# Last shared tile at the batch's end, maxima split and selection moved; router's weights written ahead of q's parts and operands

## What is computed

```python
xn = _layernorm(x)
x = x + attn(xn) + ffn(xn)
# attn: 16 heads of 8, causal softmax, output projection, then
out = jnp.where(jnp.isnan(out), 0, out)
# ffn: 8 experts of width 176, the best 2 of a softmax of logits,
combine = topk_w / (topk_w.sum(-1) + 1e-20) * 2.5
y = sum_e combine[e] * ((silu(x @ wg[e]) * (x @ wu[e])) @ wd[e])
# and a shared one of width 352, not weighted
return y + (silu(x @ swg) * (x @ swu)) @ swd
```

## Time and profile before

| | |
|---|---|
| median of 3 runs | 626.02 us (625.43 to 626.56) |
| profiled execution | 626.13 us, of which the trace's span is 624.4 us |
| PE busy | 538.2 us (86%) |
| DVE busy | 479.1 us (77%) |
| ACT busy | 349.7 us (56%) |
| POOL busy | 342.8 us (55%) |
| chain that ended last | PE 53%, DVE 17%, issue 12%, ACT 10%, POOL 4%, DMA 2% |
| TensorE's granted clock | 0.973 of full, mean |

### The profile page before, as it was taken

How to read it: one execution, slowest core, us unless ns; L and a number is a source line. 1 busy time by engine, 2 the same in 40 slices (tenths; PEclk the granted TensorE clock), 3 DMA queues, 4 the chain that set the end, 5 groups by cost and what they waited for, 6 DMA issues and landing times.

```text
span 624.4 us, 13266 instructions
## 1 busy us (share of the span) xinstructions
PE 538.2 (86%) x4568; PEld 299.7 (48%) x4568; DVE 479.1 (77%) x784; ACT 349.7 (56%) x478; POOL 342.8 (55%) x358
## 2 busy tenths in 40 slices
PE   2627989988899979998899979999899988999794
PEld 1315742655336642565436653466426653466322
DVE  5947988897968977798868978789767979589412
ACT  5412398353983459533883359633793359633591
POOL 5155734484346845387345944477354864378342
PEclk9968999998999999999999999999999999999896
DMA  8645023700345004710246004610138003530000
GB/s 272 177 154 132 2 72 120 202 3 0 123 125 163 2 21 140 196 51 0 82 135 190 0 6 136 199 66 0 62 124 214 7 3 121 169 118 3 20 1 17
DMA packets 43197, 56.65 MB, mean 91 GB/s; under 512 B 4544, under 2 KB 28576, under 8 KB 43168
## 3 DMA queue, kind: packets, MB, share of 16 engines
q1 hardware_dynamic: 40800, 53.56, 28.8%
q10 hardware_dynamic: 2368, 2.70, 1.3%
HBM read 41.05 MB, written 14.81 MB: 89 GB/s over the span
## 4 chain that ended last, share of the span: by engine, by line
PE 53%; DVE 17%; issue 12%; ACT 10%; POOL 4%; DMA 2%; SPq 0%; DVEq 0%; POOLq 0%; ACTq 0%
PE banks L608 10%; PE banks L505 7%; ACT probs L805 7%; PE banks L470 6%; PE banks L486 5%; PE banks L581 5%; DVE neg_max L1140 5%; PE banks L472 5%; PE banks L471 5%; PE banks L488 3%; PE banks L487 3%; DVE probs L1122 2%; DVE not_nan L1197 2%; POOL probs L885 2%; POOL hid_lo L891 1%
## 5 line engine op out<-in xcount | busy, mean ns | idle before, releaser
L1140 DVE TENSOR_REDUCE neg_max<-banks 128x2 f32<-128x1024 f32 (+3 forms) x224 | 195.0, 916 | 28.1 <-PE banks L496 26.4
L805 ACT ACTIVATE probs<-banks 128x1024 f32<-128x1024 f32 x160 | 155.4, 1030 | 8.1 <-PE banks L581 5.8
L891 POOL TENSOR_TENSOR hid_lo<-probs,hid_hi 128x512 fp32r<-128x512 f32 (+1 forms) x88 | 113.6, 1291 | 75.1 <-ACT hid_hi L760 75.1
L885 POOL TENSOR_TENSOR probs<-probs,cb 128x512 f32<-128x512 f32 x88 | 113.0, 1284 | 73.8 <-ACT probs L753 66.7
L919 POOL TENSOR_SCALAR_AFFINE_SELECT probs<-probs 128x512 f32<-128x512 f32 x128 | 88.8, 717 | 112.3 <-ACT probs L805 112.3
L753 ACT ACTIVATE probs<-banks 128x512 f32<-128x512 f32 (+1 forms) x112 | 66.8, 597 | 134.2 <-PE banks L472 134.2
L760 ACT ACTIVATE hid_hi<-probs 128x512 fp32r<-128x512 f32 (+1 forms) x112 | 70.4, 628 | 80.2 <-DVE probs L1122 79.9
L470 PE MATMUL banks<-x_hi,w_hi 128*128 128x512 f32 (+1 forms) x224 | 95.0, 424 | 11.7 <-DVE probs L1122 10.8
L1122 DVE TENSOR_TENSOR probs<-probs,banks 128x512 f32<-128x512 f32 (+1 forms) x112 | 75.4, 680 | 33.6 <-POOL probs L885 29.2
L608 PE MATMUL banks<-probs,v_op 128*32 128x512 f32 (+3 forms) x1024 | 95.2, 444 | 0.4
L471 PE MATMUL banks<-x_lo,w_hi 128*128 128x512 f32 (+1 forms) x224 | 88.6, 396 | 0.0
(11 more groups left out here) (120 smaller groups left out, 590.3 us busy)
## 6 DMA issues: line engine op xcount, KB each, us to landing
cb<-c_dram SPq DMA_DIRECT2D x32, 256.0 KB, 4.2
q_op<-q_dram SPq DMA_DIRECT2D x32, 192.0 KB
k_op<-k_dram SPq DMA_DIRECT2D x32, 192.0 KB
cb<-c_dram SPq DMA_DIRECT2D x16, 224.0 KB, 4.6
q_dram<-q_parts SPq DMA_DIRECT2D x8, 384.0 KB, 2.5
k_dram<-k_parts SPq DMA_DIRECT2D x8, 384.0 KB, 2.6
cb<-c_dram SPq DMA_DIRECT2D x16, 192.0 KB, 4.1
cb<-c_dram SPq DMA_DIRECT2D x16, 160.0 KB, 4.3
```

Source lines behind the costliest of these rows:

```text
L805: nc.scalar.activation(probs[:, g % 2, 2 * u:2 * u + 2, :], ring[:, at:at + 2, :], ACT.Exp).then_inc(exp_done, 1)
L885: nc.gpsimd.tensor_tensor(sg[k % 3][:, :], sg[k % 3][:, :], cb[:, TILE_ORDER[k], :], ALU.mult).then_inc(weighted, 1)
L891: nc.gpsimd.tensor_tensor(hid_lo[0:n, k % 3, :], hid[k % 3][0:n, :], hid_hi[0:n, k % 3, :].bitcast(F32), ALU.subtract).then_inc(hid_lo_don ...
L1140: return nc.vector.tensor_reduce(out, in_, AX.X, ALU.max, negate=True)
```

## The change

The NaN selection no longer touches `base` and `both`. DVE adds the experts' result into x's own place (`x_sb`). `att` is a buffer of its own, POOL sets `clean` to zero, DVE copies `att` into it where it is a number, and POOL adds `clean` to `x_sb` at the start of the next experts stage; the store of batch i - 1 stands in SP's list of batch i, ahead of the maxima. Find and copy stand on DVE at the end of attention, behind `normalise_o`, no longer ahead of the last `hidden`. Exp 0 of attention waits for that `hidden` no more.

From batch 1 on, the order of tiles is 11, 12, the eleven routed ones, 13, so the last tile is shared. On DVE the maxima are split one `hidden` later. DVE also makes the high part of the last two tiles. ACT copies k behind the first exp instead of ahead of it; PE forms the transposed scores 0 ahead of the projections of v and the logits.

DVE's and SP's orders in attention change as the rows below show. In the prologue the low parts of the routed gate and up weights are both made by DVE, v's bias has a semaphore of its own, the router's weights go out on ACT's queue, and three pairs of maxima stand ahead of `hidden` 3.

Of the diff, in the order SP, PE, ACT, POOL, DVE in experts, DVE in attention:

```diff
+TILES_FIRST = list(range(ROUTED, NT)) + list(range(ROUTED))
+TILES_LATER = list(range(ROUTED, NT - 1)) + list(range(ROUTED)) + [NT - 1]
...
             def weights_out(j):
...
                 sp.wait_ge(comb_written, 16 * j + 16)
+                apart(sp, sp_passed)
...
             def batch(i):
                 k_parts_out(i + 1)
                 q_parts_out(i + 1)
+                weights_out(i + 1)
                 operands_in(i + 1, i, 0)
-                weights_out(i + 1)
                 for m in range(len(CB_GROUPS)):
                     weights_around(m)
                 operands_in(i + 1, i, 1)
+                if not (isinstance(i, int) and i == 0):
+                    store(i - 1)
                 maxima_in(i + 1)
-                store(i)
-                sp.wait_ge(stored, 16 * i + 16)
...
...
                         if front:
                             project_k(b + 1)
+                        scores_t(b, 0, 0)
+                        if front:
                             project_v_and_logits(b + 1, vl)
-                        scores_t(b, 0, 0)
...
-                            if (g, u) == (2, 3):
+                            if (g, u) == (1, 3):
                                 transpose_comb(i + 1)
...
                     if k == NT - 2:
+                        high_hidden(b, k - 1)
                         if front:
                             take_xT(b + 1)
...
-                    if k >= 1:
+                    if 1 <= k < NT - LATE_HIGH:
                         high_hidden(b, k - 1)
+                    if i is None and k == 3:
+                        weights_out()
...
-                        if n == 0:
-                            act.wait_ge(hid_done, NT * i + NT)
...
                             if (g, u) == (0, 0):
+                                take_k(i + 1)
                                 exp_router(i + 1)
...
+                if i is not None:
+                    if not (isinstance(i, int) and i == 0):
+                        add_clean(i - 1)
+                    clear(i)
...
                 for k in range(NT + 1):
-                    if k == 4 and i is not None:
-                        add_attention(i)
-                    if k == NT and i is not None:
-                        find_numbers(i)
-                        finish_output(i)
-                    if k >= 1:
+                    if k >= 1 and not (k == 4 and i is None):
                         hidden(b, k - 1)
+                    if k >= 1 and n == NAT_ALL and pairs_at[k - 1]:
+                        split_maxima(b)
...
+                        if k == 3 and m == 1 and i is not None:
+                            add_attention(i)
                         pair(b, i, n)
                         n += 1
-                    if n == NAT_ALL and pairs_at[k]:
-                        split_maxima(b)
+                    if k == 4 and i is None:
+                        hidden(b, 3)
                     if k >= NT - LATE + 2:
+                        if k - 2 >= NT - LATE_HIGH:
+                            high_hidden(b, k - 2)
                         low_hidden(b, k - 2)
+                high_hidden(b, NT - 1)
+                low_hidden(b, NT - 1)
                 if front:
                     router_logits(b + 1, vl)
-                low_hidden(b, NT - 1)
...
                     take_v(i + 1, vl)
                     split_k(i + 1)
+                    router_weights(i + 1)
                     split_q(i + 1)
+                    take_combT(i + 1)
                 add_tokens(i)
                 if front:
-                    router_weights(i + 1)
-                    take_combT(i + 1)
                     split_x(i + 1, xnT[:, :])
...
                 normalise_o(i, 0)
                 if second:
                     statistics(3)
+                else:
+                    find_numbers(i - 1)
+                    finish_output(i - 1)
```

More of the change, by code:

```diff
@@ L77, in rows_of, with tiles_of, routed_through @@
     return LAST if tile == NT - 1 else P
+def tiles_of(b):
+    return TILES_FIRST if isinstance(b, int) and b == 0 else TILES_LATER
+def routed_through(b, k):
+    return sum(t < ROUTED for t in tiles_of(b)[:k + 1])
 def expert_segments():
@@ L445, in gate_up @@
             def gate_up(b, k):
-                tile = TILE_ORDER[k]
+                tile = tiles_of(b)[k]
                 n = rows_of(tile)
@@ L895, in experts, with clear, add_clean @@
             def experts(b, i):
-                for k in range(NT - ROUTED - 1):
-                    low_hidden(b, k)
-                if i is None:
-                    low_down()
-                place_v(b, i)
-                for k in range(NT - ROUTED, NT):
-                    if k == NT - ROUTED + 2 and i is not None:
-                        sum_all(i)
-                    for m, tiles in enumerate(CB_GROUPS):
-                        if TILE_ORDER[k] == tiles[0]:
+                tiles = tiles_of(b)
+                if i is not None:
+                    if not (isinstance(i, int) and i == 0):
+                        add_clean(i - 1)
+                    clear(i)
+                for k in range(NT):
+                    for m, group in enumerate(CB_GROUPS):
+                        if tiles[k] == group[0]:
                             pool.wait_ge(cb_loaded[m], 16 * len(SEGMENTS[m]) * (b + 1))
-                    weigh_hidden(b, k)
-                    if k - 1 < NT - LATE:
+                    if tiles[k] < ROUTED:
+                        weigh_hidden(b, k)
+                    if 1 <= k <= NT - LATE:
                         low_hidden(b, k - 1)
-            def sum_all(i):
-                pool.wait_ge(tail_step, 3 * i + 1)
-                nc.gpsimd.tensor_tensor(both[:, :, :], att[:, :, :], base[:, :, :], ALU.add).then_inc(summed, 1)
+                    if k == 2:
+                        if i is None:
+                            low_down()
+                        place_v(b, i)
+            def clear(i):
+                before(pool, summed, i)
+                apart(pool, pool_passed)
+                nc.gpsimd.memset(clean[:, :, :], 0.0).then_inc(cleared, 1)
+            def add_clean(i):
+                own = x_sb[:, bass.ds(i * QT, QT), :]
+                pool.wait_ge(tail_step, 3 * i + 3)
+                nc.gpsimd.tensor_tensor(own, own, clean[:, :, :], ALU.add).then_inc(summed, 1)
             def mask(view):
@@ L960, in _ @@
             attend(NB - 1)
-            sum_all(NB - 1)
+            add_clean(NB - 2)
+            clear(NB - 1)
         @block.vector
@@ L1032, in split_qk @@
             def split_qk(j, n, taken, parts, step, written):
-                whole, rest = qk_f[:, n, :], qk_rest[:, n, :]
+                whole, rest = qk_f[:, n, :], qk_rest[:, :]
                 dve.wait_ge(taken, j + 1)
@@ L1203, in finish_output, with add_last @@
                 apart(dve, dve_passed)
-                dve.wait_ge(summed, i + 1)
+                dve.wait_ge(cleared, i + 1)
                 apart(dve, dve_passed)
                 apart(dve, dve_passed)
-                nc.vector.copy_predicated(base[:, :, :], not_nan[:, :, :], both[:, :, :]).then_inc(tail_step, 1)
+                nc.vector.copy_predicated(clean[:, :, :], not_nan[:, :, :], att[:, :, :]).then_inc(tail_step, 1)
+            def add_last():
+                own = x_sb[:, (NB - 1) * QT:NB * QT, :]
+                dve.wait_ge(tail_step, 3 * NB)
+                dve.wait_ge(summed, NB - 1)
+                nc.vector.tensor_tensor(own, own, clean[:, :, :], ALU.add).then_inc(summed, 1)
             def pair(b, i, n):
```

91 lines of the change are left out of this document (45 added, 46 removed).

## The result

The changed kernel takes 650.6 us (648.0 to 654.1), the kernel before 625.7 on the same chip: 1.040 times as long, 95% interval 1.035 to 1.045. I had forecast 635.8 us and a range of 615 to 646. The direction was right; the size was 24.9 us instead of 9.8, and outside the range.

What follows compares the result with a forecast made beforehand. ACT paces attention, PE then PE with DVE pace experts, which end in a chain. On the 624.4 us span, - 15.1 - 2.8 - 0.2 - 5.7 + 23.1 + 10.5 = +9.8 gave 634.2, so 635.8 us measured; range 615 to 646.

Steps and rivals of the forecast that it cites:

- The mechanism of the loss: Attention: the router's instructions ahead of q's parts and the weights' write ahead of the operands make PE's first pair wait.
- the stall: PE idle ahead of its first pair, waiting for the operands: 3.3 us in each of seven batches, 23.1 us more.
- from the operands' first issue until they can be used: 8.84 us: Attention, ahead of PE's first pair: operands usable 8.84 us after first issue, as in the prologue; at most 8.81 in the loop.
- the stretch up to exp 3 of the first batch: Prologue and batch 0: 5.7 us gained in the prologue, 1.1 lost with PE's new order; 4.6 less.
- all that follows the pairs: Everything from PE's first pairs on, end of experts' gains against clock loss included: 8.7 us less.
- The prologue: Before the loop: earlier weights' write, `cb` and maxima gain 5.7 us, with bounds of 3 and 7.
- The lower bound of 3 us: Prologue: gain only 3 us if the write waits for the operands' traffic and `cb` comes at 41.7 or later.
- The clock: Behind PE's stall the granted clock falls to 0.50, costing 1.5 us in each of seven batches, 10.5 us.
- Rival 1: Behind the stall ahead of PE's first pair, the clock holds: 625.3 us, range 620 to 628; chance 16%.
- The end of experts: From the split of the maxima to exp 3: exps start earlier, 2.2 us less six times; 15.1 less together.
- `add_attention`: Moved into an idle gap of DVE in experts' PE-paced part: 0.4 us less in 7 batches, 2.8.
- Rival 2: Attention's operands come in time for PE's first pair; find and copy cost 1.4 us seven times: 612 us; chance 14%.

Runs made afterwards that it cites:

- experiment 1: Changed kernel with the attention stage back in the old order on DVE, SP and PE: 614.4 us, 0.981 of the kernel before.
- experiment 2: Changed kernel with SP's order alone undone, operands ahead of the weights' write: 639.9 us, 1.025 of the kernel before.
- experiment 4: Changed kernel with DVE's order and PE's transposition in attention undone, SP's order kept: 656.4 us, 1.047 of the kernel before.
- Experiment 3: Changed kernel with SP holding the `cb` reads until the first operands have landed: 643.6 us, 1.029 of the kernel before.
- experiment 9: Kernel before with one edit, the split of the maxima behind the last-but-one `hidden`: 614.4 us, 0.982 of the kernel before.
- experiment 10: Kernel before with the attention part of the change alone, on DVE, SP and PE: 669.7 us, 1.071 of the kernel before.
- experiment 8: From experiment 1, prologue's weights' write back on SP's queue, constants and `hidden` 3 at their old place: 613.0 us, 0.978 of the kernel before.
- experiment 11: Changed kernel with 14 unused matmuls on PE ahead of the wait for the operands: 640.1 us, 1.022 of the kernel before.
- experiment 6: From experiment 1, the split of the maxima again ahead of the last-but-one `hidden`: 628.1 us, 1.004 of the kernel before.
- experiment 7: From experiment 1, a routed tile last in every batch, as in the kernel before: 612.8 us, 0.978 of the kernel before.
- experiment 5: From experiment 1, find and copy moved from the end of attention into the first part of experts: 615.8 us, 0.982 of the kernel before.
- experiment 12: From experiment 1, the normalising of the tokens moved behind the sixth pair's place: 624.3 us, 0.997 of the kernel before.

## Why the prediction was right in direction and wrong in size

**The mechanism of the loss was right.** The stall ahead of PE's first pair stands where it was put, with a DMA as releaser. q's parts were to come 7.9 us behind exp 3 (8.16 in the batch shown, 7.4 in the mean), the operands 4.3 later (4.3). Experiments 1, 2 and 4 show both orders as its cause.

**The term that was mis-sized is the stall: 3.3 us forecast, 4.4 measured**, seven times (23.1 against 30.7 us from exp 3 to the pair). The step that failed is "from the operands' first issue until they can be used: 8.84 us". It is 10.3 in the mean of the seven batches, while q's parts come 0.5 us sooner than forecast. I took the 8.84 from rows 8 and 6, where nothing or only a small write follows the operands. In the changed order the write is ahead, so nothing holds the `cb` reads back any more, and they enter the DMA engines 3.1 us behind the operands' first issue. Experiment 3 puts them back behind and gets 8.8 us instead of 10.3. The forecast counted every instruction that was moved, but not what the moved wait had been keeping away: the write's wait on SP was the fence between operands and `cb`.

This is half of the error. On the span 9.8 us more were forecast and 24.6 measured: the seven stalls are 7.6 us of the difference, the stretch up to exp 3 of the first batch 3.5 (4.6 less forecast, 1.1 less measured), all that follows the pairs the rest (8.7 less forecast, 5.0 less measured), and this last is mainly the clock.

**The prologue: 5.7 us forecast, nothing measured.** SP's queue, ACT's queue, PE and POOL there, which answer to rows 8:

```profile
31.07 1.19 ACTq L776 DMA_DIRECT2D c_dram<-combT  x1
...
35.62 2.22 SPq L361 DMA_DIRECT2D cb<-c_dram  x5
...
37.92 0.64 PE L515 MATMUL banks<-k_op,q_op 48*64 48x384 bf16 x8 [1.15 <-DVE neg_max L1167]
42.21 1.26 POOL L903 TENSOR_TENSOR probs<-probs,cb 128x512 f32<-128x512 f32 x1 [7.66 <-DMA cb<-c_dram]
```

The write left at 31.07, as forecast, but took 4.56 us beside the operands' reads, not 2.75, and from the `cb` issue to the first product it was 6.6 us, not 5.0: POOL starts at 42.21, 0.8 us sooner than before, not at 39.3. In the ten traces with this order it starts at 42.2 to 44.4, in the kernel before and experiments 9 and 10 at 43.0 to 43.6, so not even the 0.8 us is a gain. The lower bound of 3 us, for a `cb` later than 41.7, named the case but not the price. PE's third pair did move, from 46.27 to 37.92; with POOL's first product where it was, that was worth nothing in experiment 8 (third pair at its old place behind `hidden` 3, POOL at 42.34).

The Trainium skill, page "DMA: Bandwidth & Descriptors", section "Queues, rings and completion order", gives the rule that engines take turns between queues. The measured write shows how little that is worth here. With nothing beside it the write takes 2.6 us (252.67 to 255.24), behind the reads on the same queue 4.9 to 6.3 in the kernel before, and beside them on the other queue 4.6 to 6.7 in the ten traces; in eight of these SP issues the `cb` reads, which wait for the write, within 0.1 us of the first pair, which waits for the operands. So the write landed about when the reads did, although it had a queue of its own. Why, no run shows.

**The clock: 10.5 us forecast.** The mechanism is shown by the granted clock of 0.50 to 0.74 behind the seven first pairs, and by experiment 11, where filling the wait gave back 10.5 us in all. The term was too small: 1.5 us per batch forecast, 2.2 by the batches of experiment 11 and 2.1 by experiment 10. In seven batches that is some 5 us, about what is missing behind the pairs. Rival 1, that the clock holds, is out for this kernel, where it fell seven times of seven.

**The end of experts: right in size, wrong in its causes.** 2.2 us per batch forecast, 2.05 to 2.2 in the trace. Experiments 6 and 9 show that the order of split and `hidden` is nearly all of it. The last shared tile brings nothing (experiment 7). That exp 0 no longer waits for find and copy shows at exp 0 (306.55 in experiment 6, 11.95 us behind the maxima, against 13.07), but k's copy behind it and, with find and copy in attention, the wait at the third pair take it back. In the changed kernel that loss is hidden by the stall, as forecast. `add_attention`, 2.8 us forecast, cannot be seen apart: all after the pairs is 5.0 us less, where the forecast (without the prologue and the first batch) had 8.7 less. The batch ahead of the loop has a share in that: from its first pair to the next exp 3 it takes 59.4 us, 1.1 more than before (58.3), where the loop's batches take 0.5 less (53.1 against 53.6). Its split takes 4.2 us instead of 2.4, and exp 1 starts 3.8 us behind exp 0 instead of 1.5. The long split is not the reason: experiment 1 has it as well (4.2 us), and there exp 1 starts 2.2 us behind exp 0 and the stretch takes 56.2 us. What this trace has of its own is the granted clock between the two exps, 0.58 from 163 to 167 us against 1.00 in experiment 1. Why it fell there is open.

**Rival 2** (operands in time: 612 us) is in effect experiment 1, at 614.4. Its price for find and copy, 1.4 us per batch, is more than its own numbers give (1.77 and 0.7 less 1.3 make 1.2). Measured are a wait of 1.30 us at the third pair and 1.4 us over the stretch, but the longer normalising, which the forecast did not have, is in both.

## What to carry over

When a transfer is moved ahead of another, look at what its wait had held back: the reads behind it now start sooner and share the engines with the very transfer that PE waits for. Price a transfer by a row in which the same traffic stands beside it, or keep the longer time as the likely one. And take a change with several parts apart: here two moved lines hold nearly all of the gain, and the attention part of the change cost 36 us.

## What the runs showed of the hardware

**A small instruction of DVE can last as long as a product of POOL.** The third instruction of the split, a cast of 128 x 64, takes 0.20 us in the first batch and 1.17 in the others; the subtractions around it 0.22 or 1.24. Here DVE and POOL in the changed kernel:

```profile
303.62 0.23 DVE L1184 TENSOR_TENSOR max_rest<-neg_max,max_parts 128x64 f32<-128x64 f32 x1
303.88 1.17 DVE L1187 CAST max_parts<-max_rest 128x64 bf16<-128x64 f32 x1
305.08 1.24 DVE L1189 TENSOR_TENSOR max_parts<-max_rest,max_parts 128x64 bf16<-128x64 f32 x1
...
303.69 1.30 POOL L903 TENSOR_TENSOR probs<-probs,cb 128x512 f32<-128x512 f32 x1 [0.16 <-ACT probs L764]
304.95 1.29 POOL L909 TENSOR_TENSOR hid_lo<-probs,hid_hi 128x512 fp32r<-128x512 f32 x1
306.20 1.29 POOL L903 TENSOR_TENSOR probs<-probs,cb 128x512 f32<-128x512 f32 x1
```

The cast ends at 305.05, just behind POOL's product (304.99); the subtraction at 306.32, just behind the next (306.24). In the same way the four instructions that normalise the tokens take 1.51 us where POOL is at its masks and 3.17 beside its sum and memset. The Trainium skill, page "SBUF — State Buffer", section "SBUF: two separate sides", says that DVE, in some of its operations, and POOL share a pair of ports, and that the one that starts first holds it for its whole instruction while the other waits; the trace agrees, with these numbers. It means that the split cost 3.1 us in the new place instead of 2.6, and that three edits (5, 6 and 12) cannot be priced by durations taken from elsewhere in the batch.

**A queue of its own does not keep a write clear of another queue's reads**: 4.6 to 6.7 us in ten traces, against 2.6, above.

**A wait of PE can cost twice**: once by its length, and once by the clock behind it. In otherwise equal batches a granted clock of 0.72 in the six us behind the wait went with 1.5 us more, one of 0.50 with 2.9 us more, and 3.5 us of filler that produce nothing gave back 10.5 us in seven batches.
